# Layer norm tails issued in smaller portions beside the Wld product, and behind each output tile's own work beside the FFN product

## What is computed

```python
def _rglru(x, ...):
    x = x @ Wx + bx
    gate_x = sigmoid(x @ Wgx + bgx)
    gate_a = sigmoid(x @ Wga + bga)
    a = gate_a * sigmoid(a_logit)
    xin = sqrt(1.0 - a * a) * (gate_x * x)
    h = linear_scan(a, xin, reverse)
    return h @ Wo + bo

xg = gelu(x)
y = (rglru_fwd(xg) + rglru_bwd(xg)) / 2 + x
y = gelu(y) @ ld_W + ld_b + x
x1 = layernorm(x + y)
w = (weights >= 0.0) * 2.0 - 1.0
f = clip((x1 @ w.T) * scale + bias, -100, 100)
out = layernorm(x1 + f)
```

## Time and profile before

| | us |
|---|---|
| median of 3 runs | 747.82 |
| lowest and highest | 746.96 and 750.04 |
| the profiled execution | 746.86 |
| its span on the slowest core, core 5 | 745.3 |
| spans of the 8 cores | 727.8 to 745.3 |
| PE, ACT, DVE busy in the span | 630.2, 349.6, 327.4 |

### The profile page before, as it was taken

One profiled execution on the slowest core, in us unless ns is written; L12 is line 12 of the kernel. 1 busy time (PEld: TensorE's weight loads), 2 busy tenths in 40 slices (PEclk: granted clock), 3 DMA queues, 4 the chain that ended last, 5 costly groups with the idle time before them and its releaser, 6 DMA issues.

```text
span 745.3 us, 7193 instructions; the slowest of 8 cores (727.8 to 745.3 us)
## 1 busy us (share of the span) xinstructions
PE 630.2 (85%) x2720; PEld 265.2 (36%) x2720; DVE 327.4 (44%) x191; ACT 349.6 (47%) x258; POOL 50.8 (7%) x96
## 2 busy tenths in 40 slices
PE   1449999999999999999999959998974969779660
PEld 0014444444444444444444424443321324224210
DVE  0000000005767777677672210123449338938846
ACT  2442332236787786776851110213463447747620
POOL 2010000000000000002032111000000000000000
PEclk9999999999999999999999979998997888868865
DMA  8996000001222232222459997626722000002305
GB/s 182 250 200 104 1 0 1 1 14 29 44 44 30 41 44 35 36 43 30 69 77 198 206 193 117 170 82 197 229 85 85 1 0 1 0 1 96 131 0 225
DMA packets 23217, 61.33 MB, mean 82 GB/s; under 512 B 2704, under 2 KB 2704, under 8 KB 23184
## 3 DMA queue, kind: packets, MB, share of 16 engines
q0 software_dynamic: 13248, 25.17, 22.3%
q1 hardware_dynamic: 8208, 29.42, 12.6%
q10 hardware_dynamic: 1728, 6.29, 2.8%
HBM read 75.55 MB, written 8.39 MB: 113 GB/s over the span
## 4 chain that ended last, share of the span: by engine, by line
PE 65%; DMA 14%; DVE 11%; issue 4%; ACT 4%; SPq 0%; DVEq 0%; ACTq 0%; POOLq 0%
PE psA L152 34%; PE psB L152 31%; DMA A<-x 6%; DMA A<-Wof 4%; DMA A<-Wob 3%; DVE A L944 2%; DVE A L704 2%; DVE A L757 2%; DVE A L743 1%; DVE A L838 1%; DMA out<-A 1%; DVE srbf L632 1%; DMA A<-Wffn 1%; ACT srbf L629 1%; DVE srows L612 1%
## 5 line engine op out<-in xcount | busy, mean ns | idle before, releaser
L152 PE MATMUL psA<-A 128*128 128x512 bf16 x1536 | 361.9, 394 | 61.0 <-ACT A L329 21.2
L152 PEld LDWEIGHTS psA<-A 128*128 128x128 bf16 x1536 | 151.3, 100 | 266.2 <-issue 101.2
L152 PE MATMUL psB<-A 128*128 128x512 bf16 x1024 | 226.8, 380 | 1.0 <-DVE A L568 1.0
L152 PEld LDWEIGHTS psB<-A 128*128 128x128 bf16 x1024 | 100.3, 98 | 122.8 <-issue 2.9
L429 DVE TENSOR_SCALAR A<-A,dvec_sb 128x2048 f32<-128x2048 f32 x16 | 20.6, 1286 | 168.0 <-ACT A L425 168.0
L440 DVE TENSOR_TENSOR A<-A 128x2048 f32<-128x2048 f32 x16 | 36.7, 2292 | 51.0 <-ACT A L433 51.0
L573 ACT ACTIVATE A<-A,dvec_sb 128x1024 bf16<-128x1024 f32 x16 | 18.4, 1148 | 79.5 <-DVE A L568 79.5
L152 PE MATMUL psB<-A,ones_sb 128*1 128x512 bf16 x128 | 37.4, 436 | 14.7 <-DVE A L950 12.0
L425 ACT ACTIVATE A<-psB,vecs_sb 128x2048 f32<-128x2048 f32 x16 | 31.5, 1967 | 31.9 <-PE psB L152 31.9
L431 ACT ACTIVATE A<-A 128x2048 f32<-128x2048 f32 x16 | 30.6, 1910 | 23.8 <-DVE A L429 23.8
L568 DVE SCALAR_TENSOR_TENSOR A<-psA,A 128x1024 f32<-128x1024 f32 x8 | 9.8, 1224 | 70.6 <-PE psA L152 58.5
(11 more groups left out here) (59 smaller groups left out, 354.9 us busy)
## 6 DMA issues: line engine op xcount, KB each, us to landing
A<-x SPq DMA_DIRECT2D x40, 512.0 KB, 7.9
A<-x ACTq DMA_DIRECT2D x8, 512.0 KB, 14.7
A<-Wof POOLq DMA_DIRECT2D x16, 256.0 KB, 10.8
A<-Wob POOLq DMA_DIRECT2D x16, 256.0 KB, 12.8
A<-Wffn SPq DMA_DIRECT2D x8, 512.0 KB, 6.0
out<-A SPq DMA_DIRECT2D x8, 512.0 KB, 3.9
A<-Wxf POOLq DMA_DIRECT2D x8, 256.0 KB, 32.0
A<-Wxb POOLq DMA_DIRECT2D x8, 256.0 KB, 22.0
```

Source lines behind the costliest of these rows:

```text
L152: inst = e.matmul(oa, lh, rh, start=st, stop=sp)
```

## The change

It has two parts, and both only change where steps of a tail are issued.

```diff
--- before.py
+++ after.py
@@ -827,7 +827,7 @@
                 pending_stats.pop(0)()
             if h == 0 and sgn_q:
                 sgn_prep(sgn_q.pop(0))
-            drain_bg(6)
+            drain_bg(4)
             xsl = o % 4
             bd.op("scalar",
                   lambda e, sl=sl, xsl=xsl: e.activation(u_ap[sl], xc56_ap[xsl],
@@ -924,10 +924,6 @@
                                   k == 0, k == CH - 1))
                     treads.append([x1B[k], sgnB])
             bd.mm_group(tiles, treads, group_reads=(), writes=[PS[slot]])
-            while len(bg) > max(0, 6 - 2 * (o // 2)):
-                bg.pop(0)()
-            if not bg and deferred:
-                deferred.pop(0)()
             bd.op("scalar",
                   lambda e, slot=slot, sl=sl, o=o:
                   e.activation(u_ap[sl], ps_ap(slot, 0, 1024), AF.Relu,
@@ -956,6 +952,10 @@
                 reads=[r2bfB[o]], writes=[rsqS[o]], inc="sc"))
             if o >= 2:
                 sq_ops.pop(0)()
+            while len(bg) > max(0, 6 - 2 * (o // 2)):
+                bg.pop(0)()
+            if not bg and deferred:
+                deferred.pop(0)()
 
             def _sum(o=o):
                 stats_tiles(lambda k, t: r2bf_ap8[k][:, t * 512:(t + 1) * 512],
```

## The result

| | before | changed |
|---|---|---|
| median of 10 runs, us | 748.18 | 760.18 |
| lowest and highest | 744.79 and 750.04 | 755.18 and 762.61 |
| the profiled execution | 746.86 | 755.18 |
| its span, slowest core | 745.3 (core 5) | 753.6 (core 4) |
| PE busy, DVE busy, ACT busy | 630.2, 327.4, 349.6 | 624.5, 327.5, 349.3 |

The ratio of the changed kernel to the one before is 1.0163, with a 95% interval of 1.0137 to 1.0190. The three engines have the same instructions as before; what grew is the time in which they wait.

The account below looks back on a forecast made before the run. PE's product stream was taken to set the time, with DVE nearly full in the rest of each FFN half. 746.86 - 8.7 + 18.7 = 756.9, plus 0.96 to the median: 757.8 us, 1.3% more; range 752.0 to 761.5.

Parts of the forecast that it names:

- First part, gain 8.7: Second Wld half: with portions of 4, tile 7 starts at 588.5, not 597.16; gain 8.7 us, bounds 6.8 to 10.5.
- tile 5 runs slow: Second Wld half: after a new 5 us PE pause, tile 5 runs at half clock, taking 5.42 us instead of 3.56.
- Second part, the chain 7.8 and 7.9 late: FFN halves: L612 waits behind tile 0's product, clips, residual and cast, starting 7.8 and 7.9 us late.
- The wait of 1.5 before residual 2: Each FFN half: DVE waits 1.5 us for tile 2's clips, a wait the pair of applies used to cover.
- The early residual pays nothing back: FFN halves: doing residual 0 early gains nothing, since it lay in DVE's wait for tile 1 anyway.
- No table load: FFN, ACT: no table load of 1.28 us comes between the clips and Ln; cost 18.7, otherwise 21.3.
- The sum: Whole kernel: gain 8.7 in the Wld stage against cost 9.3 + 9.4 = 18.7 in the FFN halves; 757.8 us.
- the time from L612 to tile 1's clips "stays": FFN halves: from L612 to tile 1 the 11.7 us stay, so tile 1 is late by as much as L612.
- the Wld hole closes whole: Rival, second Wld half: tile 4's 13.8 us are kept to the end, 752.7 or 749.7 us; 12 in 100.
- DVE absorbs the late start: Rival, FFN halves: late chain is hidden by DVE work, 739.1 us; a gain once a half costs under 4.35; 6 in 100.
- the first part gives nothing: Rival, second Wld half: the new hole costs as much as the old one, 766.5 us; 4 in 100.

Follow-up runs that it names:

- where the part stood alone: Kernel before with only portions of 4 steps, not 6, in the second Wld half, FFN stage as before: 741.32 us, ratio 0.9851.
- the run of that portion alone: Kernel before with only the portion at tile 0 of each FFN half moved behind the tile's own work: ratio 1.0162, L612 span +15.7 us.
- the run with the portion between the two: Kernel before with only tile 0's FFN portion moved, to between ACT's clips and DVE's residual: 763.63 us, ratio 1.0175.
- where it stood alone: Kernel before with only the later FFN portions (three pairs of applies) moved behind the tile's own work: 754.21 us, ratio 1.0019.
- the second part's 19.8: Kernel before with all FFN portions behind the tile's own work, Wld stage as before, second run: 767.57 us, ratio 1.0263, L612 span +19.8 us.

## Why the prediction was right, and where it was short

**First part, gain 8.7: right.** 8.8 in the mean of the cores between the first two L612, where the part acts, and 8.4 over the whole stretch. The walk was exact as far as DVE sets the pace: tile 5 was to come 30.9 us behind L605 (575.9 less 545.0) and does. That tile 5 runs slow was right too; it takes 5.6 us in the changed kernel and 6.2 where the part stood alone, not 5.42.

**Second part, the chain 7.8 and 7.9 late: right.** L612 is 8.27 behind tile 0 in both halves of the changed kernel, 7.93 and 8.03 more than before, and the run of that portion alone costs 15.7. That ACT's clip and not DVE carries most of it is shown by the run with the portion between the two.

**The wait of 1.5 before residual 2: right.** 1.42 in the trace, 3.3 in all where it stood alone. The early residual pays nothing back, as argued: DVE waits 5.42 before residual 1.

**No table load: right.** In the changed kernel Ln starts at 602.53 on ACT, 1.30 behind L612 (601.23), as in the earlier trace rows.

**The sum was 2 us short.** 10.0 were forecast, 12.0 and 11.5 measured. What was mis-sized is the step that the time from L612 to tile 1's clips "stays". It was read from core 5 alone. Two terms are in it. The broadcasts: 11.83 on all cores now, against a mean of 11.58 and 11.52 before, 0.6 us in both halves; core 5 had 11.84 before already, so its rows could not show it. Tile 1: 12.35 us for both halves against 11.41, 0.9 us, part of which may be chance (above). Another 0.3 is L612, 15.96 late in the two halves and not 15.7. The last 0.3 to 0.4 lies behind tile 1's clips: up to the next L612, with the later L612 taken off, it is 1.9 us more in the first half and 1.4 in the second, where 1.5 each were forecast. The first part took 0.1 off by giving 8.8. That makes the 2.0. Core 5 was among the two slowest cores of the eight in these halves (54.8 and 55.1 between L612, where cores 0 to 4 and 7 had 53.3 to 53.8), so against its rows the change looked cheaper than against the mean. The part behind tile 1's clips shows it. PE on core 0 of the kernel before, the burst of small sums at the end of the first FFN half:

```profile
636.09 5.62 PE L152 MATMUL psB<-A,ones_sb 128*1 128x512 bf16 x18 [0.92 <-DVE A L950]
```

and in the changed kernel on core 4:

```profile
650.96 6.52 PE L152 MATMUL psB<-A,ones_sb 128*1 128x512 bf16 x18 [5.93 <-DVE A L946]
```

while core 5 needed 6.98 for the same burst before. That a core which is already slow there loses less when the pauses grow is argued from this, and not tested.

**The rivals.** That the Wld hole closes whole is out: 4.95 us of it came back before tile 5. That DVE absorbs the late start is out: a half costs 9.9 us (half of the second part's 19.8), far over the 4.35 at which it would turn. That the first part gives nothing is out by its own run.

## What to carry to other kernels

An operation that waits for a long product, put at the head of an in-order queue, holds everything behind it; if that is a chain on which the product after the next depends, the chain should start first and only its last steps stand behind the next product. Background work on the engine that frees the PSUM slots should be dealt out so that one portion fits under one tile, never two. Read a change's price from several cores: here, on core 5, the broadcasts already took 11.84 us, so its rows hid the 0.4 that the change cost a half on most others.

## What the runs showed of the chip

Filling a pause of 9.5 us with products did not keep the clock for the tile behind it: with PE busy and at 2.4 GHz to 613 us, six microseconds of broadcasts with waits of 2.20 and 0.73 between them were followed by 0.50 in the next window. And the eight cores of one execution, which run the same program on sequences of the same shape, stand in different places of this pattern: tile 1's wait for its clips was 4.86 on one core and 6.45 on another in one execution. What decides which core gets which was not found.
